# A graph-attention layer on one core: where two-input vector operations and the input loads are placed

## The reference

```python
feats = einsum('bnf,hfo->bhno', x, kernel)
scores = einsum('hbnd,hbdm->hbnm', einsum('bnf,hfd->hbnd', x, att), einsum('bnf,hfd->hbdn', x, att2))
m = adj * scores
m = where(m >= 0, m, 0.2 * m) / 4.0 + where(adj == 0, -1e9, 0)
attn = softmax(m, axis=-1) * where(adj == 0, 0, 1)
y = x + relu(einsum(attn, feats) + bias)
out = (y - mean(y)) / sqrt(var(y) + 1e-5)     # over the 64 columns
```

## Time and profile before

| | |
|---|---|
| three runs | 950.94 us median (948.58 to 952.34) |
| profiled execution | 947.27 us, span 945.5 us |
| PE busy | 848.3 us (90%) |
| DVE busy | 812.7 us (86%) |
| ACT busy | 786.8 us (83%) |
| POOL busy | 637.9 us (67%) |
| mean granted TensorE clock | 0.97 of full |

### The profile page before, as it was taken

One profiled execution on the slowest core, in us unless ns is written; L12 is line 12 of the kernel. 1 busy time (PEld: TensorE's weight loads), 2 busy tenths in 40 slices (PEclk: granted clock), 3 DMA queues, 4 the chain that ended last, 5 costly groups with the idle time before them and its releaser, 6 DMA issues.

```text
span 945.5 us, 14871 instructions
## 1 busy us (share of the span) xinstructions
PE 848.3 (90%) x4668; PEld 257.1 (27%) x4668; DVE 812.7 (86%) x1509; ACT 786.8 (83%) x1553; POOL 637.9 (67%) x547
## 2 busy tenths in 40 slices
PE   4088998999999999989998999989999999899994
PEld 3022332232223322222222322223223332222131
DVE  3076899989998899979998799978999789999994
ACT  2076998998898988988988988979889799899993
POOL 5064886767875778847877578757687477777453
PEclk9578999999999999999999999999999999999997
DMA  8892778837875769719588387775697376972001
GB/s 235 133 279 57 211 116 214 205 79 182 166 205 132 182 121 246 187 31 232 104 220 205 70 191 144 202 156 144 133 199 200 87 210 101 247 188 47 18 1 36
DMA packets 198403, 144.58 MB, mean 153 GB/s; under 512 B 177104, under 2 KB 177104, under 8 KB 198320
## 3 DMA queue, kind: packets, MB, share of 16 engines
q1 hardware_dynamic: 195152, 139.91, 63.0%
q10 hardware_dynamic: 3168, 3.67, 2.4%
HBM read 94.08 MB, written 12.51 MB: 113 GB/s over the span
## 4 chain that ended last, share of the span: by engine, by line
PE 58%; DVE 21%; issue 8%; DMA 5%; ACT 4%; SPq 2%; POOL 1%; POOLq 0%; DVEq 0%; ACTq 0%
PE z L511 33%; PE numer L542 21%; DVE z L830 11%; DMA x_sb<-in_x 4%; DVE probs L830 3%; ACT probs L741 2%; PE misc L446 2%; DMA edges<-in_adj 1%; PE misc L486 1%; ACT squares L682 1%; DVE nwt L901 1%; DVE yb L874 1%; SPq L236 1%; DVE rstd L905 1%; PE misc L439 1%
## 5 line engine op out<-in xcount | busy, mean ns | idle before, releaser
L830 DVE SCALAR_TENSOR_TENSOR z<-z,maskT 128x512 f32<-128x512 f32 (+1 forms) x864 | 555.9, 678 | 76.4 <-PE z L511 70.8
L511 PE MATMUL z<-self_st,other_st 96*128 96x512 bf16 (+3 forms) x2016 | 533.7, 381 | 42.5 <-issue 24.8
L381 POOL TENSOR_TENSOR probs<-probs,lows 128x512 f32<-128x512 f32 (+1 forms) x288 | 358.9, 1247 | 280.1 <-ACT probs L735 272.7
L741 ACT ACTIVATE probs<-z 128x512 f32<-128x512 f32 (+1 forms) x864 | 464.1, 598 | 74.5 <-PE z L511 64.5
L542 PE MATMUL numer<-probs,vals 128*32 128x512 f32 (+1 forms) x2304 | 304.0, 600 | 5.7 <-ACT o_sb L689 3.3
L511 PEld LDWEIGHTS z<-self_st,other_st 96*128 96x128 bf16 (+1 forms) x2016 | 165.7, 98 | 516.0 <-ACT probs L741 222.8
L734 ACT ACTIVATE lows<-z 128x512 f32<-128x512 f32 (+1 forms) x288 | 175.7, 610 | 52.2 <-DVE probs L830 50.4
L830 DVE SCALAR_TENSOR_TENSOR probs<-z,maskT 128x512 f32<-128x512 f32 (+1 forms) x288 | 191.4, 665 | 27.6 <-PE z L511 27.6
L735 ACT ACTIVATE probs<-probs 128x512 f32<-128x512 f32 (+1 forms) x288 | 184.9, 642 | 0.0
L339 POOL TENSOR_SCALAR mask<-edges 128x1500 int16<-128x1500 f32 x96 | 139.1, 1449 | 9.9 <-DMA edges<-in_adj 2.2
L542 PEld LDWEIGHTS numer<-probs,vals 128*32 128x32 f32 x2304 | 45.8, 108 | 99.1 <-ACT probs L741 72.4
(11 more groups left out here) (71 smaller groups left out, 281.5 us busy)
## 6 DMA issues: line engine op xcount, KB each, us to landing
edges<-in_adj SPq DMA_DIRECT2D x88, 750.0 KB, 5.9
parts_dram<-part SPq DMA_DIRECT2D x21, 384.0 KB, 2.7
self_st<-parts_dram SPq DMA_DIRECT2D x42, 192.0 KB, 5.5
other_st<-parts_dram SPq DMA_DIRECT2D x42, 192.0 KB, 5.9
edges<-in_adj SPq DMA_DIRECT2D x8, 468.8 KB
x_sb<-in_x SPq DMA_DIRECT2D x8, 352.0 KB
out<-cent SPq DMA_DIRECT2D x8, 352.0 KB
maskT<-mask SPq DMA_TRANSPOSE x96, 6.0
```

Source lines behind the costliest of these rows:

```text
L381: pool.tensor_tensor(p, p, lows[:, g % 2, 0:WIDTH[st]], ALU.mult).then_inc(pooled, 1)
L511: return nc.tensor.matmul(z[:, v % BUFS * STEP + i, 0:WIDTH[st]], other_st[par][rows, h, c * P:(c + 1) * P], self_st[par][rows, h, st * W: ...
L741: nc.scalar.activation(slot, bank, ACT.Exp, scale=LOW).then_inc(expd, 1)
L830: return nc.vector.scalar_tensor_tensor(out, z[:, v % BUFS, 0:WIDTH[st]], FLOOR, maskT[(par + st) % 2][:, c, 0:WIDTH[st]], ALU.max, ALU.mult)
```

## The change

It has five parts. (1) `finish` keeps the strip's rows in PSUM: the division and the bias are done in place in `misc`, and step 5 reads them there and x from SBUF, so no step reads two SBUF tensors; the bank is freed by step 5 instead of step 3. (2) Newton's nine steps become twelve operations of 128 x 12 on POOL (`refine`), four behind each of tiles 7, 9 and 10 of the last strip; DVE keeps the three seed steps, now behind v = 47, 48 and 49; `scale_rows` moves from tile 7 to tile 10, `center` from tile 9 to 8. (3) `x_sb` has a third buffer; SP issues the load of b + 1 at the start of batch b, ahead of strip 0's transposes. (4) The preparation rounds, finish steps, masks and splits stand at other units and tiles. (5) The test in `norms` is one operation with the second factor as scalar operand, in the place of three.

```diff
+XB = 3
...
 ROOT_STEPS = 3
-ROOT = 3 + 3 * ROOT_STEPS
-NEWTON = NS + ROOT - 1
+SEED = 3
+ROOT = 4 * ROOT_STEPS
+NEWTON = NS + SEED - 1
...
-PREP_AT = [36, 40, 44, 48, 52, 76, 80, 120, 124]
...
-FINISH_AT = (None, 16, 19, 22, 25, 28, 31, 34, 46)
+FINISH_AT = (None, 16, 19, 21, 23, 25, 29, 31, 44)
...
-MASKS_AT = ({0: 0, 1: 1, 2: 2, 3: 3}, {0: 0, 1: 1, 2: 2, 3: 3}, {3: 0, 4: 1, 5: 2, 6: 3})
-SPLITS_AT = ({}, {4: (0, 1), 5: (2,), 6: (3,), 7: (4,), 8: (5,), 10: (6, 7), 11: (8,)}, {0: (9,), 1: (10,), 2: (11,)})
+MASKS_AT = ({0: 0, 1: 1, 2: 2, 3: 3}, {2: 0, 3: 1, 4: 2, 5: 3}, {3: 0, 4: 1, 5: 2, 6: 3})
+SPLITS_AT = ({}, {0: (0, 1), 1: (2,), 6: (3,), 7: (4,), 9: (5,), 10: (6, 7), 11: (8,)}, {0: (9,), 1: (10,), 2: (11,)})
 SHIFT_AT = 5
-SCALE_AT = 7
-CENTER_AT = 9
-ROOT_EVERY = 4
+REFINE_AT = {7: range(0, 4), 9: range(4, 8), 10: range(8, 12)}
+SCALE_AT = 10
+CENTER_AT = 8
+ROOT_EVERY = 1
...
-        x_sb = [sb(f"x_sb{p}", [P, NT, F], F32) for p in range(2)]
+        x_sb = [sb(f"x_sb{p}", [P, NT, F], F32) for p in range(XB)]
...
@@ -291,6 +294,11 @@
                 with sp.Else():
                     sp.sem_inc(big_adj_in, 16 * NT)
                     sp.sem_inc(shift_in, 16 * 3)
+                if not last:
+                    if b >= 2:
+
+                        sp.wait_ge(misc_free, use(b - 1, OUT_PLACE[0]) + 1)
+                    load_x(b + 1, (b + 1) % XB)
                 for st in range(NS):
 
                     if not (last and st == NS - 1):
@@ -304,9 +312,6 @@
                                 load_edges(b, st + 2, j)
                             elif not last:
                                 load_edges(b + 1, st + 2 - NS, j)
-                    if st == 0 and not last:
-                        sp.wait_ge(resid, at(b, NS, 1))
-                        load_x(b + 1, 1 - par)
                     if st == 1 and not last:
                         for k in range(3):
                             stack(1 - par, k, at(b, SPLITS, SPLITS), at(b, 48, 48))
@@ -402,8 +407,25 @@
                 pool.wait_ge(centered, at(b, NS, st + 1))
                 pool.tensor_tensor(sq[:, :, :], rows, rows, ALU.mult).then_inc(squared, 1)
 
+            def refine(steps, b):
+
+                v, y, t = vs[:, :], rstd[:, :], nwt[:, :]
+                for k in steps:
+                    if k == 0:
+                        pool.wait_ge(seeded, b + 1)
+                    else:
+                        pool.wait_ge(refined, at(b, ROOT, k))
+                    if k % 4 == 0:
+                        pool.tensor_tensor(t, y, y, ALU.mult).then_inc(refined, 1)
+                    elif k % 4 == 1:
+                        pool.tensor_tensor(t, t, v, ALU.mult).then_inc(refined, 1)
+                    elif k % 4 == 2:
+                        pool.tensor_scalar(t, t, -0.5, 1.5, ALU.mult, ALU.add).then_inc(refined, 1)
+                    else:
+                        pool.tensor_tensor(y, y, t, ALU.mult).then_inc(refined, 1)
+
             def scale_rows(b, par):
-                pool.wait_ge(rstd_ready, at(b, 1, 1))
+                pool.wait_ge(refined, at(b, ROOT, ROOT))
                 pool.tensor_tensor(cent[par][:, :, :], cent[par][:, :, :],
                                    rstd[:, :].unsqueeze(2).broadcast_to([P, NT, HF]), ALU.mult).then_inc(normed, 1)
 
@@ -422,6 +444,8 @@
                                 split(k, at(b, SPLITS, SPLITS))
                         if c == SHIFT_AT and st == 0 and not last:
                             zero_shift(b, par, first)
+                        if c in REFINE_AT and st == NS - 1 and not first:
+                            refine(REFINE_AT[c], b - 1)
                         if c == SCALE_AT and st == NS - 1 and not first:
                             scale_rows(b - 1, 1 - par)
                         if c == CENTER_AT and not (first and st == 0):
@@ -429,6 +453,7 @@
 
             batches(batch)
             center(B, 0, -1)
+            refine(range(ROOT), B - 1)
             scale_rows(B - 1, 1)
 
         @block.tensor
@@ -593,7 +618,7 @@
                                 r = PREP_AT.index(v)
                                 if r == 0:
                                     pe.wait_ge(x_in, at(b, 32, 64))
-                                prep_round(1 - par, r, use(b, PREP_PLACE[r]))
+                                prep_round((b + 1) % XB, r, use(b, PREP_PLACE[r]))
                             if v % SV == OUT_AT and not (first and v == OUT_AT):
                                 k = v // SV
                                 pe.wait_ge(numer_free, at(b, NS, k + 1))
@@ -777,13 +801,9 @@
                                          flag_f[0:1, 0:2 * H].rearrange("p (k h) -> p k h", h=H),
                                          axis=AX_X).then_inc(flag, 1)
                     dve.wait_ge(flag, flags + 1)
-                    nc.vector.tensor_tensor(flag_f[0:1, 2 * H + 2:2 * H + 3], flag_f[0:1, 2 * H:2 * H + 1],
-                                            flag_f[0:1, 2 * H + 1:2 * H + 2], ALU.mult).then_inc(flag, 1)
-                    dve.wait_ge(flag, flags + 2)
-                    nc.vector.tensor_scalar(flag_f[0:1, 2 * H + 3:2 * H + 4], flag_f[0:1, 2 * H + 2:2 * H + 3],
-                                            1.0 / 16, SAFE * SAFE, ALU.mult, ALU.is_le).then_inc(flag, 1)
-                    dve.wait_ge(flag, flags + 3)
-                    nc.vector.tensor_copy(safe[buf][0:1, 0:1], flag_f[0:1, 2 * H + 3:2 * H + 4]).then_inc(safe_ready, 1)
+                    nc.vector.tensor_scalar(safe[buf][0:1, 0:1], flag_f[0:1, 2 * H:2 * H + 1],
+                                            flag_f[0:1, 2 * H + 1:2 * H + 2], 16.0 * SAFE * SAFE,
+                                            ALU.mult, ALU.is_le).then_inc(safe_ready, 1)
 
             def large_tile(b, t, rows, steps, adj_in):
 
@@ -850,35 +870,35 @@
                     dve.memset(slot, 0.0).then_inc(raised, 1)
 
             def finish(step, st, b, par, misc_n):
-                buf, t0 = par if st >= 0 else 1 - par, st % NS * SJ
+                buf, t0 = (b if st >= 0 else b - 1) % XB, st % NS * SJ
                 summed = misc[:, 0:SJ * P].rearrange("p (j c) -> p j c", c=OW)
                 if step == 1:
                     dve.wait_ge(misc_full, misc_n)
                     nc.vector.tensor_scalar(den[:, :], summed[:, :, D], 1e-30, None, ALU.max).then_inc(epi, 1)
                 elif step == 2:
-                    dve.wait_ge(epi, at(b, 4 * NS, 4 * st + 1))
+                    dve.wait_ge(epi, at(b, 5 * NS, 5 * st + 1))
                     nc.vector.reciprocal(rden[:, :], den[:, :]).then_inc(epi, 1)
                 elif step == 3:
-                    dve.wait_ge(epi, at(b, 4 * NS, 4 * st + 2))
-                    nc.vector.tensor_tensor(ob[:, :, :].rearrange("p j (h d) -> p (j h) d", d=D),
-                                            summed[:, :, 0:D],
+                    dve.wait_ge(epi, at(b, 5 * NS, 5 * st + 2))
+                    nc.vector.tensor_tensor(summed[:, :, 0:D], summed[:, :, 0:D],
                                             rden[:, :].unsqueeze(2).broadcast_to([P, SJ * H, D]),
-                                            ALU.mult).then_inc(misc_free, 1)
+                                            ALU.mult).then_inc(epi, 1)
                 elif step == 4:
+                    dve.wait_ge(epi, at(b, 5 * NS, 5 * st + 3))
+                    rows = summed[:, :, 0:D].rearrange("p (j h) d -> p j h d", h=H)
+                    nc.vector.tensor_tensor(rows, rows, bias_rep[:, :].rearrange("p (h d) -> p h d", d=D).unsqueeze(1)
+                                            .broadcast_to([P, SJ, H, D]), ALU.add).then_inc(epi, 1)
+                elif step == 5:
+                    dve.wait_ge(epi, at(b, 5 * NS, 5 * st + 4))
+                    nc.vector.scalar_tensor_tensor(yb[:, :, :].rearrange("p j (h d) -> p (j h) d", d=D),
+                                                   summed[:, :, 0:D], 0.0,
+                                                   x_sb[buf][:, t0:t0 + SJ, :].rearrange("p j (h d) -> p (j h) d", d=D),
+                                                   ALU.max, ALU.add).then_inc(misc_free, 1)
+                elif step == 6:
                     dve.wait_ge(misc_free, misc_n + 1)
-                    nc.vector.tensor_tensor(ob[:, :, :], ob[:, :, :],
-                                            bias_rep[:, :].unsqueeze(1).broadcast_to([P, SJ, HF]),
-                                            ALU.add).then_inc(epi, 1)
-                elif step == 5:
-                    dve.wait_ge(epi, at(b, 4 * NS, 4 * st + 3))
-                    nc.vector.scalar_tensor_tensor(yb[:, :, :], ob[:, :, :], 0.0,
-                                                   x_sb[buf][:, t0:t0 + SJ, :], ALU.max,
-                                                   ALU.add).then_inc(resid, 1)
-                elif step == 6:
-                    dve.wait_ge(resid, at(b, NS, st + 2))
```

(43 more changed lines are left out.)

## The result

The changed kernel takes 914.23 us in the median (910.71 to 916.41, 4 runs), the kernel before 949.76 us beside it (947.07 to 952.34, 4 runs). The ratio is 0.962 (95% interval 0.958 to 0.967): faster by 35.5 us, as forecast in sign, 11 us slower than the forecast's 903, and inside its range of 886 to 926. The profiled execution has a span of 910.8 us.

What follows compares the result with a forecast made beforehand. No engine is near the span; undisturbed, ACT fills each 2.62 us group, so waits were targeted. Gains 26.9 + 18 + 11.2 + 3, losses 7 + 2 + 1.5 + 1.1: 47.5 off 947.3, plus 3.7 to the median, 903 us; range 886 to 926.

Steps and rivals of the forecast that it cites:

- Newton off DVE: Nine operations leave DVE with their waits for POOL: 26.9 us gained over seven batches.
- The seed stays exposed: Two of DVE's three one-input seed steps held up by POOL, 0.5 us each in seven batches: 7 us lost.
- Finish steps: Division, bias and residual on DVE lose their waits for POOL: 3 us gained for the whole run.
- Step 7: The mean in finish, moved from unit 34 to 31, can wait for POOL in strip 1: 2 us lost.
- The bank: `misc`, freed three units ahead of preparation rounds 0, 5 and 7, makes TensorE wait: 1.5 us lost over 21 rounds.
- The rival with 25 us: TensorE waits 1.2 us for the `misc` bank in each of 21 rounds: 25 us back, 927; chance 0.17.
- x: Loading x a batch early removes TensorE's 15.1 us wait and some slow clock: 18 us gained, bounds 10 and 20.
- The norms: Last norm round three units behind DVE's maximum, fewer small operations: 1.6 us in each of seven batches, 11.2 us gained.
- POOL's refinement: Twelve small POOL operations at 0.25 us each with the gap, hidden in the batches; about 1.1 us lost in the tail.
- The rival with POOL as the bound: Tiles 7 to 11 of strip 2 overfill POOL if small operations cost as much as the multiply: 984; chance 0.04.
- Masks, splits, center: The same POOL work at other tiles, at most 2.7 us a group, costs nothing.
- Step 5 of the prediction: The term on the early x load: SP's queue behind it is late by two short issues, with ten groups of room.

Runs made afterwards that it cites:

- e11: e1 with the mean (finish step 7) back at unit 34, center at tile 9 and the three seed steps at units 45 to 47: 887.62 us, ratio 0.934.
- e1: Changed kernel with masks and splits of strip 1 back at the tiles of before: 892.66 us, ratio 0.938.
- e8: Kernel before with only the third x buffer and the early load of x: 927.46 us, ratio 0.975.
- e12: e11 with POOL's refinement six operations each at tiles 7 and 8, and scale_rows at tile 8 instead of 10: 891.58 us.
- e5: Changed kernel with only the masks of strip 1 back at tiles 0 to 3, splits at the new tiles: 895.02 us, ratio 0.941.
- e2: Changed kernel with three x buffers, but x loaded at its old place behind strip 0's transposes and edge loads: 977.55 us, ratio 1.028.

## Why the prediction was right, and which step failed

1. *Newton off DVE* (26.9 us): right. From copy to copy the second strip lost 3.7 us in each middle batch and 3.9 in the last. By itself the move gave 21: in its trace the x wait is 6.6 us longer, and the last strip and the tail 3.1.
2. *The seed stays exposed* (7 us lost): the step is held up as said, but the price was wrong. One of three steps waits in each of seven batches, not two (L919 0.70 to 0.86 us in six, L914 1.13 in the seventh), and the groups around it are as long as in the first batch, which has none (15.2 us for five): it costs next to nothing. ACT's last copies of the preparation lie beside it.
3. *Finish steps* (3 us gained): 4 measured, with their own move of units in it. *Step 7* (2 us lost): it waits, but in strip 2, where I had it covered by the norm's maximum, not in strip 1: L902 stands behind the maximum and takes 1.10 us still. Its price was too low: moving it away made two groups of each batch 0.7 us shorter, which is most of the 5 us of e11 against e1. The rule of the Trainium skill (SBUF — State Buffer, section "SBUF: two separate sides"), by which a one-input operation in a two-port mode is held up too, agrees with these rows: 1.10 and 0.86 us instead of 0.16. The reciprocal and the sums, also with one SBUF input, never vary (0.244 and 0.41 us).
4. *The bank* (1.5 us lost): TensorE's weight loads wait 2.9 us each in rounds 5 and 7, 5.8 in all, at most 0.4 a time, where the kernel before already had 4.7 us of such waits. The rival with 25 us fell. (Its 927 lies 1 us outside the range that was to hold it.)
5. *x* (18 us gained, at most 20): right in mechanism and near in size: 19.4 by the profiled executions, from which the term was worked out, and 24 by the medians. The kernel before varies by 8 us from run to run there (947.1 to 955.2), e8 by 0.7.
6. *The norms* (11.2 us): oversized, 7 measured, since I took the removal of the wait and of the operations as standing in the same group, and the test's remaining three came back later. The sign "the norms' group below 4 us" failed in the changed kernel (4.18), where the mean stands in that group, and held without it (3.17).
7. *POOL's refinement*: 0.21 us each, 0.29 with the gap, against my 0.25. The tail is 0.9 us longer (15.2 against 14.3 us from the last copy), as forecast with 1.1, though the prediction's own figures (12 x 0.25 less 9 x 0.17) give 1.5. Not forecast: the last strip is 1.7 us longer (30.2 against 28.5 from copy to copy); there `scale_rows` at tile 10 stands ahead of the last multiplies, and with it at tile 8 (e12) 0.8 of it is gone. The rival with POOL as the bound needed 1.02 us; it fell.
8. *Masks, splits, center: "nothing; their cover is the lateness allowed in 7"*. This is the step that failed. It was argued for POOL alone. The masks also set when SP may issue the transposes and the next batch's edge loads, and SP issues in order: two tiles later there put the loads, 3 MB, next to the writes of the parts, and SP's waits for those next to the masks of the following batch. The masks cost 19 us (914.23 against 895.02 of e5), more than the forecast was off. Step 5 of the prediction had looked at SP's queue for the x load and found ten groups of room, at the start of the batch; the shortage is at the end of it.

Without this loss the sum of 903 would have been 8 us too high (e5), not 11 too low: the seed's 7 us were not lost, and x gave more than 18 by the medians, against which step 7 cost more than 2 and the norms gave less than 11.2. That the forecast is off by 11 us and not by 19 is luck: two errors of opposite sign. A slip that changes nothing: 945.5 / 8 is 118 and not about 115; steady batches take 109 to 113 us in the trace, which is where the "other 17 us" come from. Of the prediction's signs, the strips of 33 to 34 us (33.3, and 33.0 in the last batch) and the end of the x wait held; "no half clock in the middle" did not, because the mask's wait brought it back.

## What to carry to other kernels

When work is moved on an in-order queue, follow each instruction that it releases onto the next queue, up to the last DMA: here a POOL operation that was hidden on POOL released four transposes and four loads on SP, and these stood in front of a write that SP waits for. When several waits are taken out of a pipeline, ask for each transfer how much of its lead time was the wait; a load that was just in time becomes the next bound (the x wait of e2). And a version that beats both was in the same edits: the change with its masks where they were, and the small one-input operations moved off POOL's multiply.

## What the runs showed of the hardware that was not expected

A `tensor_scalar` of 4 columns (L902) takes up to 1.10 us instead of 0.16 when it starts inside one of POOL's operations, and ends with it, while a sum over 256 columns inside such a multiply takes its 0.41 us: how little an operation reads does not save it. Nor is the name enough: the test, a `tensor_scalar` of one element with its second factor as scalar operand (L804), takes 0.20 us inside POOL's square, as it does without one. A 384 KB write that lands in 2.7 us in the median of the kernel before lands in 7.0 in the changed one; by e5's order, waits of 7.0 us right behind the edge loads and 2.3 us with 7.3 us of distance, it is the transfers just ahead of it that make the difference. And a wait costs more than its length: around the wait of 4.44 us at 160.15 four groups take 16.6 us, where they take 10.6 in e1, and the clock stays at its lower level for 5.2 us after TensorE has work again. Over the run, 15.8 us of waiting for the mask go with 19.9 us of span (910.8 against 890.9).
